# Two-layer decoder on one core: the third attention's key products moved into the first mixture's first wait, and filling products added in other waits

## The reference, cut to what matters

```python
x = x + L0_attn(ln(x))          # gated delta rule, 2 heads of 128, a triangular inverse per sequence
x = x + L0_xattn(ln(x), ctx)    # first attention: tanh layers, 16 heads of 16, softmax over ctx
x = x + L0_ffn(ln(x))           # first mixture: 4 experts of width 512, norm inside, top 2, norm outside
x = x + L1_attn(ln(x))          # second attention: one latent of 128, causal
x = x + L1_xattn(ln(x), ctx)    # third attention: q from ln(x), k = ctx @ wk, v = ctx @ wv, causal
x = x + L1_ffn(ln(x))           # second mixture: 8 experts of width 128, gelu, top 2
```

## Time and profile before

| | |
|---|---|
| median of 3 runs | 5358.99 us |
| the profiled execution, its own time | 5357.75 us |
| its span, first to last instruction | 5355.9 us |
| PE busy | 4674.5 us (87%) |
| DVE busy | 4123.0 us (77%) |
| POOL busy | 3977.9 us (74%) |
| ACT busy | 2322.0 us (43%) |
| mean granted clock of TensorE | 0.964 |
| the chain that ended last: PE, DVE, ACT | 62%, 21%, 6% of the span |

### The profile page before, as it was taken

The page is one execution under the profiler, slowest core; times in us unless marked ns, Lnnn a source line. Parts: engine busy times, 40 slices in busy tenths (PEclk is TensorE's granted clock), DMA queues, the critical chain, the costliest instruction groups (busy, mean ns, idle before and its releaser), DMA issues.

```text
span 5355.9 us, 108285 instructions
## 1 busy us (share of the span) xinstructions
PE 4674.5 (87%) x28201; PEld 3065.9 (57%) x28362; DVE 4123.0 (77%) x11313; ACT 2322.0 (43%) x4480; POOL 3977.9 (74%) x12365
## 2 busy tenths in 40 slices
PE   1089999989999998999999998998999999899999
PEld 0065656656565565656556565665656566565655
DVE  8868787777878777777787877778777877777778
ACT  0044444444444444443444544445444444444444
POOL 6688685868858587785858868586895858678585
PEclk7599999999999999999999999999999999999999
DMA  3000000000000000000000000000000000000000
GB/s 90 12 9 9 21 1 25 5 9 21 9 21 1 25 6 9 21 1 29 1 13 17 9 21 1 25 5 13 17 9 21 1 25 5 9 21 7 15 1 17
DMA packets 61911, 78.34 MB, mean 15 GB/s; under 512 B 11168, under 2 KB 53808, under 8 KB 61232
## 3 DMA queue, kind: packets, MB, share of 16 engines
q1 hardware_dynamic: 52784, 62.42, 3.5%
q10 hardware_dynamic: 8448, 8.39, 0.5%
HBM read 45.04 MB, written 8.46 MB: 10 GB/s over the span
## 4 chain that ended last, share of the span: by engine, by line
PE 62%; DVE 21%; issue 8%; ACT 6%; POOL 2%; DMA 0%; DVEq 0%; ACTq 0%; SPq 0%; POOLq 0%
PE bank L1266 7%; PE bank L1299 5%; PE bank L1185 5%; PE bank L1171 5%; PE bank L1359 4%; PE bank L1197 4%; PE bank L1385 4%; PE bank L1219 3%; PE bank L1093 3%; PE bank L1100 3%; DVE smax L1892 2%; DVE arena L1502 2%; PE bank L1284 2%; ACT arena L856 2%; PE bank L1206 2%
## 5 line engine op out<-in xcount | busy, mean ns | idle before, releaser
L1892 DVE TENSOR_REDUCE smax<-bank 128x4 f32<-128x512 f32 x768 | 524.3, 683 | 77.9 <-PE bank L1171 30.0
L843 ACT ACTIVATE arena<-bank 128x512 f32<-128x512 f32 x768 | 454.9, 592 | 241.7 <-PE bank L1185 235.8
L1896 DVE TENSOR_TENSOR arena<-bank,smax 128x512 f32<-128x512 f32 x768 | 530.7, 691 | 26.4
L1185 PE MATMUL bank<-ident,arena 128*128 128x128 f32 x3072 | 485.1, 280 | 48.9 <-ACT arena L830 31.2
L509 POOL TENSOR_TENSOR arena<-arena 128x1024 f32<-128x1024 f32 x17 | 32.2, 1894 | 657.2 <-DVE y_nat L1624 657.1
L1266 PE MATMUL bank<-w,arena 128*128 128x512 f32 x1024 | 497.2, 617 | 14.0 <-DVE arena L1834 14.0
L1185 PEld LDWEIGHTS bank<-ident,arena 128*128 128x128 f32 x3072 | 344.5, 141 | 250.0 <-ACT arena L832 82.3
L1171 PE MATMUL bank<-arena 64*128 64x512 f32 x1536 | 433.6, 641 | 50.9 <-DVE arena L1941 13.5
L1299 PE MATMUL bank<-w,arena 128*128 128x256 f32 x2048 | 454.1, 380 | 13.9 <-ACT arena L902 13.9
L830 ACT ACTIVATE arena<-arena,rstd 128x512 f32<-128x512 f32 x512 | 368.3, 719 | 209.6 <-DVE arena L1896 203.9
L1299 PEld LDWEIGHTS bank<-w,arena 128*128 128x128 f32 x2048 | 387.9, 190 | 90.2 <-issue 22.5
(11 more groups left out here) (439 smaller groups left out, 11787.1 us busy)
## 6 DMA issues: line engine op xcount, KB each, us to landing
arena<-in_x_dram SPq DMA_DIRECT2D x35, 512.0 KB, 3.6
xn_next<-arena SPq DMA_DIRECT2D x17, 512.0 KB, 2.9
arena<-cum_dram SPq DMA_DIRECT2D x17, 512.0 KB, 3.8
arena<-in_ctx_dram SPq DMA_DIRECT2D x16, 512.0 KB, 3.8
out_dram<-arena ACTq DMA_DIRECT2D x16, 512.0 KB, 3.1
xn<-xn_next SPq DMA_DIRECT2D x15, 512.0 KB, 2.9
w<-in_L_ffn_w_dram SPq DMA_DIRECT2D x8, 512.0 KB
w<-in_L_ffn_w_dram SPq DMA_DIRECT2D x1, 1024.0 KB
```

The lines of the kernel that those rows point to most:

```text
L843: act.activation(PT[:, v % 2], bank[3 + v % 2][:, :].rearrange("p (h q) -> p h q", h=QH), ACT.Copy).then_inc(S["pt"], 1)
L1185: ins = tr(bank[3 + v % 2][:, j * P:(j + 1) * P], Ssb[:, v % 4, j, :], ident[:, :])
L1892: dve.tensor_reduce(smax[:, u, :], sc, AX, ALU.max).then_inc(S["s_max"], 1)
L1896: dve.tensor_tensor(Ssb[:, u % 4], sc, smax[:, u, :].unsqueeze(2).broadcast_to([P, QH, P]), ALU.subtract).then_inc(S["s_sub"], 1)
```

## The change

The key products of the third attention are taken from their place behind the second attention and put in place of `keep_busy(8, 4)` in the first mixture; they go to banks 4 and 5. ACT copies each half to a free half unit of the large buffer (`k_third`), and PE's first two transposes of z, which write the same banks, wait for those copies. ACT later makes the third attention's masked keys from `k_third` instead of from PSUM. The value products are split into halves around the transposes. Filling products are added at eight places, and the counts of semaphores that shift are adjusted.

```diff
--- before.py
+++ after.py
@@ -54,7 +54,7 @@
     MT=2, IT=2, V_psum=2, Vb=2, lev0=2, lev=12, inv_eye=2, W_psum=10, W=10, U_psum=10, U=10,
     T_psum=10, T=10, v1_psum=2, v1=2, c_psum=2, c_add=2, vnew_psum=2, vnew=2, oT_psum=2, oT=2, y0_psum=2,
 
-    h_psum=6, h_act=6, lat_psum=1, lat=1, q_psum=6, q=6, k_psum=5, k_rows=1, km=6, v_psum=5, v=6,
+    h_psum=6, h_act=6, lat_psum=1, lat=1, q_psum=6, q=6, k_psum=5, k_rows=1, km=8, v_psum=5, v=6,
     s_psum=48, s_max=48, s_sub=48, p_exp=48, t_psum=48, pt=48, pv=48, o_sb=12, otr_psum=12,
     o_rec=12, o_norm=12, attT_psum=12, attT=12, y_psum=6,
 
@@ -200,6 +200,7 @@
         QT = cut(8, C, N)
         KM = cut(0, G, C, QH, P)
         V2 = cut(19, G, NH, 2 * HD)
+        k_third = [arena[:, 3 * G * D + N:4 * G * D], arena[:, 12 * G * D + N:13 * G * D]]
         smax = sb("smax", [P, QUADS, QH])
         Ssb = cut(21, 4, QH, P)
         PT = cut(11, 2, QH, P)
@@ -850,7 +851,10 @@
 
                 def key_masks(a_no, c, src, bias):
 
-                    act.wait_ge(S["k_psum"], at(it, "k_psum", (0, 2, 3)[a_no] + c + 1))
+                    if bias:
+                        act.wait_ge(S["k_psum"], at(it, "k_psum", c + 1))
+                    else:
+                        act.wait_ge(S["km"], at(it, "km", 7 if c else 4))
                     for j in range(QH):
                         if bias:
                             ins = act.activation(KM[:, :, c, j, :], heads(src[:, :]), ACT.Identity, scale=halfmask[:, j:j + 1], bias=halfbias[:, j:j + 1])
@@ -860,7 +864,7 @@
 
                 def latent_masks():
 
-                    act.wait_ge(S["k_psum"], at(it, "k_psum", 3))
+                    act.wait_ge(S["k_psum"], at(it, "k_psum", 5))
                     for m in range(2):
                         two = slice(2 * m, 2 * m + 2)
                         for j in range(QH):
@@ -892,6 +896,10 @@
                     act.activation(ulg[:, :], uparts[:, 2, :], ACT.Ln, scale=-2.0).then_inc(S["up_log"], 1)
                     act.wait_ge(S["up_log"], at(it, "up_log", e + 1))
                     act.activation(urs[:, :], ulg[:, :], ACT.Exp, scale=-0.5).then_inc(S["up_rstd"], 1)
+                    if e == 0:
+                        for c in range(C):
+                            act.wait_ge(S["k_psum"], at(it, "k_psum", 2 + c + 1))
+                            act.activation(k_third[c], bank[4 + c][:, :], ACT.Copy).then_inc(S["km"], 1)
                     if e == 1:
                         key_squares(it, 1, moved_next, xn_next)
                     if e == 2:
@@ -918,9 +926,9 @@
                 attention(1)
 
 
-                key_masks(2, 0, bank[2], False)
+                key_masks(2, 0, k_third[0], False)
                 xT_copy(4)
-                key_masks(2, 1, bank[3], False)
+                key_masks(2, 1, k_third[1], False)
                 half_rstd(4)
                 attention(2)
 
@@ -1033,6 +1041,8 @@
                     for c in range(C):
                         for g in range(G):
                             if c == 0 and s > 0:
+                                if s == 5 and g == 2:
+                                    keep_busy(3, 2)
                                 pe.wait_ge(S["xn"], at(it, "xn", s - 1 + g + 1))
                             ins = tr(bank[XT_BANKS[s][c]][:, g * P:(g + 1) * P], (xn if s else xn0)[:, g, c * P:(c + 1) * P], ident[:, :])
                         ins.then_inc(S["xT_psum"], 1)
@@ -1116,6 +1126,7 @@
                             ins.then_inc(S["T_psum"], 1)
                             if l == 0:
                                 context(h)
+                                keep_busy(3, 4)
 
                 pe.wait_ge(S["Vb"], at(it, "Vb", 2))
                 for h in range(DH):
@@ -1257,6 +1268,7 @@
 
 
                 residual_features(2, 2, 3, 5)
+                keep_busy(3, 5)
                 xT_ready(2)
 
                 def up(e, g):
@@ -1272,7 +1284,10 @@
                     for c in range(C):
                         ins = mm(bank[7][:, g * E0:(g + 1) * E0], xT[:, c, g * P:(g + 1) * P], rgb[:, c, 0, :], start=(c == 0), stop=(c == C - 1))
                 ins.then_inc(S["r_psum"], 1)
-                keep_busy(8, 4)
+                for m in range(C):
+                    for c in range(C):
+                        ins = mm(bank[4 + m][:, :], wk[:, c, m * P:(m + 1) * P], ctxT[:, c, :], start=(c == 0), stop=(c == C - 1))
+                    ins.then_inc(S["k_psum"], 1)
                 for e in range(E0):
                     for k in range(KC0):
                         n = e * KC0 + k
@@ -1280,6 +1295,8 @@
                             pe.wait_ge(S["z"], at(it, "z", 4 * (e + 1)))
                         if n >= 2:
                             pe.wait_ge(S["zT"], at(it, "zT", n - 1))
+                        else:
+                            pe.wait_ge(S["km"], at(it, "km", 2 + n + 1))
                         for g in range(G):
                             ins = tr(bank[4 + n % 2][:, g * P:(g + 1) * P], z[:, e % 2, g, k * P:(k + 1) * P], ident[:, :])
                         ins.then_inc(S["zT_psum"], 1)
@@ -1304,10 +1321,12 @@
                 key_features(it, 1)
                 beta_columns(it, 1)
                 residual_features(3, 4, MIX_FILL, 2)
+                keep_busy(4, 2)
                 xT_ready(3)
                 for c in range(C):
                     ins = mm(bank[2][:, :], Wcd[:, c, :], xT[:, c, :], start=(c == 0), stop=(c == C - 1))
                 ins.then_inc(S["lat_psum"], 1)
+                keep_busy(2, 6)
                 pe.wait_ge(S["lat"], at(it, "lat", 1))
                 for g in range(G):
                     ins = mm(bank[7][:, g * 2 * HD:(g + 1) * 2 * HD], latT[:, g * P:(g + 1) * P], Wkv[:, :], start=True, stop=True)
@@ -1323,17 +1342,17 @@
 
 
 
-                for m in range(C):
-                    for c in range(C):
-                        ins = mm(bank[2 + m][:, :], wk[:, c, m * P:(m + 1) * P], ctxT[:, c, :], start=(c == 0), stop=(c == C - 1))
-                    ins.then_inc(S["k_psum"], 1)
+                def third_values(m):
+
+                    for g in (2 * m, 2 * m + 1):
+                        for c in range(C):
+                            ins = mm(bank[4 + m][:, (g % 2) * D:(g % 2 + 1) * D], ctxT[:, c, g * P:(g + 1) * P], wv[:, c, :], start=(c == 0), stop=(c == C - 1))
+                    ins.then_inc(S["v_psum"], 1)
+
+                third_values(0)
                 pe.wait_ge(S["res"], at(it, "res", 8))
                 residual_features(4, 6, 0, 5)
-                for g in range(G):
-                    for c in range(C):
-                        ins = mm(bank[4 + g // 2][:, (g % 2) * D:(g % 2 + 1) * D], ctxT[:, c, g * P:(g + 1) * P], wv[:, c, :], start=(c == 0), stop=(c == C - 1))
-                    if g % 2:
-                        ins.then_inc(S["v_psum"], 1)
+                third_values(1)
                 xT_ready(4)
                 for m in range(C):
                     for c in range(C):
@@ -2133,7 +2153,7 @@
 LN_EXP_TABLE = "natural_log_exp_and_others"
 HIGH_BITS = -4096
 SPLIT = 4097.0
-MIX_FILL = 14
+MIX_FILL = 18
 INPUT_ROUND = 6
 NORM_ROUND = 9
 ROUTER_ROUND = 25
@@ -2150,7 +2170,7 @@
 SET_RGB = 4
 SET_ROUTER = 15
 SET_DVE = 29
-KM_BEFORE = (0, 2, 4)
+KM_BEFORE = (0, 4, 6)
 S_BANKS = (0, 1, 2, 6)
 XT_BANKS = ((6, 7), (0, 1), (2, 6), (0, 1), (0, 1), (0, 1))
 
```

## The result

The changed kernel took **5276.04 us**, the median of 4 runs (5273.18 to 5279.19), against 5358.99 (5348.94 to 5359.26): a ratio of 0.985, 95% interval 0.9833 to 0.9867. The forecast was 5255, with 5234 to 5304. So the sign and the range held, and the gain is 83 us where the sum gave 103.

The account below looks back on a forecast made before the run. It took PE, 87% busy, as the bound, losing time to waits and low-clock stretches. Terms 54.9 + 25.1 + 13.0 + 9.3 + 7.6 + 3.2 - 10.1 = 103.0 us off 5357.75 gave 5255, range 5234 to 5304.

Parts of the forecast that it names:

- The inverse: Two groups of three fills at L1115 keep the clock full: 1.55 us in 6 iterations, 9.3 us.
- The mixture: First mixture, real products in the wait for z: short length, 1.67 us less in 15 iterations, 25.1 us.
- The key products and the latent stage: Keys moved from behind the second attention: 3.43 us x 16, 54.9; fills at L1309: 1.85 us in 7 iterations, 13.0.
- everything from the transposes on keeps its shape: Third attention: what follows the transposes stays as it was and comes 3.43 us earlier in each iteration.
- The gates: Six fills before the second mixture's gates: 1.09 us in 7 iterations, 7.6; full clock 0.2 us x 16, 3.2.
- The products down: Experts' products down: low clock in half the iterations, 6 more than the 2 before, a loss of 10.1 us.
- The fills and the copies at no cost: 25 new fills fit their waits with 0.1 to 0.4 us spare; ACT's key copies and masks stay hidden: 0.
- the one on POOL: `au` is ready 11.9 us before its read, 5 remain; rival that POOL becomes the bound: near 5280, chance 0.02.
- Keys alone: Rival: the clock falls as often as before and only the moved key products gain, 54.9 us: 5303, chance 0.15.
- Fills on the path: Rival: all 25 fills outlast their waits, 0.22 us each, with no clock gain: 5391, chance 0.02.
- key products exposed: Rival: values don't cover DVE's addition, or masks delay xT's copy; half the keys' gain, 27, goes: 5280, chance 0.08.
- No slow stretch at all: Rival: the products down keep their full clock too: 5241, chance 0.10.

Follow-up runs that it names:

- experiment 4: The kernel before with the 25 new fills alone, the key products and eight old fills left in place: 5315.73 us, ratio 0.992.
- the early copy: An edit: DVE copies `a_row` two score tiles sooner in the third attention; in the changed kernel 5252.99 us, ratio 0.9807 to the kernel before.
- experiment 11: The changed kernel measured once more, with no edit: 5278.53 us, ratio 0.9863 to the kernel before.
- experiment 3: The changed kernel with all 25 added fills taken out, so the moved keys alone: 5305.34 us, ratio 0.9905 to the kernel before.
- experiment 1: The changed kernel with DVE's copy of `a_row` issued two score tiles sooner: 5252.99 us, ratio 0.9807 to the kernel before.
- experiment 7: The changed kernel with the early copy and both halves of the value products ahead of the transposes: 5305.97 us, ratio 0.9901 to the kernel before.
- experiment 2: The changed kernel with one redundant decay step before DVE's copy, making it 0.2 us later: 5306.54 us, ratio 0.9907 to the kernel before.
- experiment 10: The changed kernel without the 25 fills and with the early copy: 5305.61 us, ratio 0.9912 to the kernel before.

## Why the prediction was right, and where it wasn't

The profiled execution gained 81.9 us (5357.75 - 5275.85), where the sum gave 103.0. Term by term, from the sums over the sixteen iterations:

- **The inverse**: 9.1, forecast 9.3. Right.
- **The mixture**: 22.4, forecast 25.1. It takes 81.0 and not 80.83, in all. Right in mechanism; experiment 4 shows that the fills ahead of it would do 15.9 of it without the keys.
- **The key products and the latent stage**: 43.1, forecast 54.9 + 13.0 = 67.9. The head of the third attention gave its 54.9 exactly (124.2 to 69.3 us), and the latent stage 8.9 of 13.0. The step "everything from the transposes on keeps its shape" failed: from the queries to the gates it is 781.7 us instead of 760.9, 20.8 more. 17 of these are the six blocked copies, the rest goes with DVE's L1564 under POOL's operation (0.33 us for 0.16) in the other ten. With the early copy the whole term is 58.4, so 15.3 of the missing 24.8 come back. What the latent stage lacks is 0.27 us in each iteration (44.51 for 44.24), and it looks like the same thing in the second attention. Two operations of DVE there, of 128x256 with two inputs from the large buffer, run beside POOL's short operations and take 0.66 and 0.69 us (L1522), where the short iterations before had 0.54 and 0.47 (L1502). PE's L1238 waits 0.44 us behind them in all sixteen, where the short ones before had a wait of 0.11 at most. That POOL is the cause there is argued from the overlap alone.
- **The gates**: 7.1, forecast 7.6 + 3.2. Nearly the whole 1.09 of a long iteration came (22.00 to 20.95). The 0.2 for the full clock was wrong: with the clock at 1.00 the stage takes the same 20.95 us as at 0.92. The argument that stood beside it, that DVE's decays end when they end, would have given 0, and I took 0.2 against it.
- **The products down**: 0, forecast -10.1. Two long ones, as before. In experiment 11 the eight came that I had assumed, at nearly the same total. The number can't be forecast from one profile.
- **The fills and the copies at no cost**: right. No wait has grown right behind them, and the masks took 2.54 us instead of 2.42 in their own cover.

**The step that failed** is the one on POOL. I worked out that `au` would still be 5 us ahead of its reader; it is 6.8 (2392.14 to 2398.97). But I asked only whether POOL's result would be late, and not what POOL does then. The earlier trace rows give `au` and its readers, and the 9.3 us of operations that POOL has behind `au`, the long one last, were in the same timeline. Within the slack of 11.9 us POOL's longest operation started 5.10 us ahead of DVE's copy (2429.91 and 2435.01) and was over before it. The change took 5.1 us out of the slack, and that put the two starts 0.02 us apart. To read a slack by its sign alone was the mistake.

That 5276 lies in the range owes something to luck. The 20.8 us in the third attention stood in no term. The 10.1 us that I had put down for the products down didn't come in this execution and made room for half of them.

**The rivals.** Keys alone has its own experiment, 5305 against a forecast 5303, but the agreement is chance: the rival had 54.9 us from the keys and no gain in clock, and in experiment 3 the mixture gained 23 us by its clock, the stretch from the latent product to the gates 23 instead of 54.9, and the inverse, the gates and the products down 6 together. Fills on the path, key products exposed, and nothing changed are excluded by the timelines above. No slow stretch at all (5241) wasn't reached: in the profile of experiment 1 the clock still falls at the gates in most iterations, for nothing, and twice at the products down. POOL did become what costs time, though not as the bound that the rival had, but as the neighbour of an instruction that shares its ports.

## What to carry to other kernels

When a change shortens the way between two engines that run free of each other, list what each of them does in the time that shrinks, not only whether the value handed over is still early: a long GpSimd operation that used to end just ahead of a VectorE step now lies on it. The median time of a group of small VectorE operations can hide this; the longest shows it, 1.90 us against 0.17 here. Look at the other small operations beside it too: with the keys alone it was another step that was held, and a place that was free in one version wasn't in the next. Where two operations of these engines start within tenths of a microsecond, a shift of one small instruction to a place with room is worth testing; here it gave 23 us of 5276. And a stage without a wait to spare can pay for a short block twice, once as the delay (1.6 us here) and once as the clock behind it (1.5 more).

## What the runs showed of the hardware

- A VectorE operation on 2 to 10 columns that starts under a GpSimd operation of 128x1024 (1.89 us) is held until that one ends: a copy 0.17 to 1.90 us, an operation with two inputs in SBUF 0.16 to 1.89, a 128x8 addition 0.16 to 1.39 (experiment 7), a 128x10 operation with a scalar 0.16 to 1.17 (experiment 11). In experiment 11 a subtraction with one of its inputs in PSUM (L1916 at 4277.12), wholly under the same operation, kept its 0.69. When VectorE started 0.02 us ahead, the copy took its usual 0.17.
- The order of two starts 0.02 us apart differed between the iterations of one execution (POOL ahead in 6, DVE in 10), and in another execution of the same kernel POOL came 0.1 to 0.87 us later. So it came out with 6 or with 0 blocked copies, at medians 2.5 us apart.
- PE's clock fell to 1.2 GHz for 6.8 us behind a wait of 1.78 us in the third attention in 5 of 6 cases, and in experiment 2 behind waits of 1.84 to 1.98 us in 14 of 15. Behind waits of 1.04 to 1.07 us at the same place (experiment 7) it stayed at 2.4 GHz in all sixteen. With filling products in waits of about 1 us the latent stage kept 2.4 GHz in all iterations (44.5 us in experiment 1), where without them it took 45.4 to 48.4 (experiment 10); 25 of them were worth 29 to 52 us.
